# A masked cross-attention stage on one core: scores and side jobs share three PSUM banks instead of two and one, and a group's row maxima are turned one tile later

## What is computed

```python
def _L1_xattn_ref(q, k, v, mask, wq_w, wq_b, wk_w, wk_b, wv_w, wv_b, fo_w, fo_b):
    qp = (q @ wq_w.T + wq_b).reshape(N, -1, HEADS, HEAD_DIM)      # q: layernorm(x), 4 x 512 x 256, 16 heads of 16
    kp = (k @ wk_w.T + wk_b).reshape(N, -1, HEADS, HEAD_DIM)      # k, v: the context, 4 x 1601 x 256
    vp = (v @ wv_w.T + wv_b).reshape(N, -1, HEADS, HEAD_DIM)
    energy = jnp.einsum('nqhd,nkhd->nhqk', qp, kp)
    energy = jnp.where(mask == 0, jnp.float32(-1e+20), energy)
    attention = jax.nn.softmax(energy / np.float32(np.sqrt(EMBED)), axis=3)
    out = jnp.einsum('nhql,nlhd->nqhd', attention, vp).reshape(N, -1, EMBED)
    return out @ fo_w.T + fo_b
```

## Time and profile before

| | us |
|---|---|
| runs of the kernel before (3) | 2139.68, 2140.29, 2343.99; median 2140.29 |
| the profiled execution's own time | 2148.22 |
| its span in the trace | 2146.3 |
| masked attention in that span | 1103.3 to 1912.2 |
| PE busy over the span | 2006.8 (93%) |
| DVE, ACT, POOL busy over the span | 1270.2, 813.8, 527.3 |

### The profile page before, as it was taken

How to read it: one execution, slowest core, us unless ns; L and a number is a source line. 1 busy time by engine, 2 the same in 40 slices (tenths; PEclk the granted TensorE clock), 3 DMA queues, 4 the chain that set the end, 5 groups by cost and what they waited for, 6 DMA issues and landing times. The chain is left out here.

```text
span 2146.3 us, 27320 instructions
## 1 busy us (share of the span) xinstructions
PE 2006.8 (93%) x10237; PEld 1102.4 (51%) x10346; DVE 1270.2 (59%) x2541; ACT 813.8 (38%) x1631; POOL 527.3 (25%) x454
## 2 busy tenths in 40 slices
PE   8989999999999999899989999999999999974994
PEld 5666567746676567746643333333333343333773
DVE  5424764366544764477777777777777777641343
ACT  3412111211112111121127666666666766750221
POOL 4311001300010000000053132235324521326664
PEclk9999999999999999999999999999999999986997
DMA  8753000200011000200236473354335432224986
GB/s 284 210 199 109 0 1 17 70 10 1 1 37 45 1 1 11 46 16 31 31 103 111 132 213 65 79 134 107 89 70 145 103 56 39 64 71 147 257 186 157
DMA packets 101530, 184.97 MB, mean 86 GB/s; under 512 B 38151, under 2 KB 62549, under 8 KB 100120
## 3 DMA queue, kind: packets, MB, share of 16 engines
q1 hardware_dynamic: 83000, 153.24, 26.9%
q0 software_dynamic: 18400, 30.00, 6.0%
HBM read 127.38 MB, written 65.25 MB: 90 GB/s over the span
## 5 line engine op out<-in xcount | busy, mean ns | idle before, releaser
L2203 DVE CUSTOM_DVE_ANT_0 ps<-ps,maskN 128x801 f32<-128x801 f32 x480 | 468.4, 1014 | 179.8 <-PE ps L1987 174.2
L2176 ACT ACTIVATE d_prob<-ps 128x512 f32<-128x512 f32 (+1 forms) x832 | 460.5, 597 | 248.1 <-PE ps L2020 242.1
L856 PE MATMUL ps<-vx_or_keys,b_xT 128*128 128x512 f32 x512 | 240.3, 597 | 4.9 <-DVE val_or_prob L1209 4.9
L840 PE MATMUL ps<-oxB,og_or_pT 128*128 128x256 f32 x1024 | 241.1, 380 | 0.0
L2019 PE MATMUL ps<-maskT,identb 128*128 128x512 bf16 (+1 forms) x577 | 222.7, 386 | 1.9 <-ACT d_prob L2176 0.9
L2032 PE MATMUL ps<-d_prob,vaug 128*32 128x512 f32 (+1 forms) x1664 | 224.0, 604 | 0.3 <-ACT d_prob L2176 0.3
L840 PEld LDWEIGHTS ps<-oxB,og_or_pT 128*128 128x128 f32 x1024 | 190.5, 190 | 37.4 <-issue 11.2
L2019 PEld LDWEIGHTS ps<-maskT,identb 128*128 128x128 bf16 (+1 forms) x658 | 64.8, 99 | 260.0 <-ACT d_prob L2176 195.3
L1095 ACT ACTIVATE prob_or_gate<-ps,b_mx 128x512 f32<-128x512 f32 (+3 forms) x128 | 66.0, 524 | 289.5 <-DVE b_mx L1200 289.5
L260 POOL DMA_INDIRECT table<-xr,slot x128 | 127.8, 998 | 192.0 <-PE ps L2020 159.8
L1209 DVE TENSOR_TENSOR val_or_prob<-ps,b_gm 128x512 f32<-128x512 f32 x128 | 88.5, 691 | 107.0 <-PE ps L856 106.9
(11 more groups left out here) (321 smaller groups left out, 2801.9 us busy)
## 6 DMA issues: line engine op xcount, KB each, us to landing
c_rawT<-in_maskT SPq DMA_DIRECT2D x24, 512.0 KB
vx_or_keys<-k_parts SPq DMA_DIRECT2D x60, 200.1 KB, 7.3
k_parts<-x_k SPq DMA_DIRECT2D x16, 600.4 KB
table<-xr POOLq DMA_DIRECT2D x16, 578.0 KB
e_buf<-table SPq DMA_DIRECT2D x32, 289.0 KB
raw<-in_mask SPq DMA_DIRECT2D x10, 800.5 KB, 4.2
vx_or_keys<-in_D_w SPq DMA_DIRECT2D x12, 640.0 KB
e_w<-in_D_w SPq DMA_DIRECT2D x12, 640.0 KB
```

The lines of the kernel that those rows point to most:

```text
L840: mm = pe.matmul(ps[:, 6 + t // 2, (t % 2) * D:(t % 2 + 1) * D], og[:, e, t * P:(t + 1) * P], oxB[:, p, e, :], start=first and t % 2 == 0, ...
L856: mm = pe.matmul(ps[:, bank, :], xTB[:, c, t * P:(t + 1) * P], vxB[:, c, h, :], start=c == 0, stop=c == NC - 1)
L2176: nc.scalar.activation(prob[0:w, T % 2, h, :], ps[0:w, BANKS[GH * T + h], :], ACT.Exp, scale=SCALE_C).then_inc(exped, 1)
L2203: v.tensor_tensor_reduce(banks, banks, maskN[:, t, MO[half]:MO[half] + w], 1.0, -3.0e38, ALU.add, ALU.max, mp[:, t, h, half:half + 1]).the ...
```

## The change

`misc_jobs` and `score_plan` go, `bank_plan` takes their place: it walks through the stage in PE's order and gives each score and each side job the bank of 0, 1 and 3 (in group 15 also 6 and 7) whose last use began longest ago. A score or a job then waits for whatever reads that bank last: the exponential of the score, or the ACT or DVE read of the side job. With nothing between, score u of the stage waits for the exponential of score u - 3. After a side job that takes a bank behind tile i, scores 0 and 1 of tile i + 1 wait for the exponentials of scores 2 and 3 of tile i, and score 2 of tile i + 1 takes the job's bank and waits for the job's reads. ACT or DVE write a mask only into a bank that PE has written whole since its last side job; otherwise PE does. Walked through, the plan has the same numbers as before: 658 masks by PE, 150 by ACT, 24 by DVE. Group 15's first two scores use banks 6 and 7.

The one semaphore `freed` is split by reader (`freed_a`, `freed_v`). The waits of PE for `l_sub`, `carried` and the copy of "x" that guarded bank 3 stand now where the bank is used again. Two waits go: of score 2 of tile 11 for the last maximum's reduction, and of a group's second maximum for the exponentials. `turn_maxima` moves from behind score 3 of tile 11 to behind score 1 of tile 12.

```diff
+def bank_plan():
+    banks, before, masks, jobs, count, whole = [], [], [], {}, {"act": 0, "dve": 0}, set()
+    used, freed_by, reads, time = {}, {}, {"a": 0, "v": 0}, 0
+    def take(G, reader, after):
+        nonlocal time
+        bank = min((0, 1, 3) if G < NGB - 1 else (0, 1, 3, 6, 7), key=lambda x: used.get(x, x - 10))
+        free = freed_by.get(bank)
+        used[bank], freed_by[bank], time = time, (reader, after), time + 1
+        return bank, free
+    def job(G, name, reader, n=1):
+        bank, free = take(G, reader, reads[reader] + n)
+        whole.discard(bank)
+        jobs[name] = (len(jobs), bank, free, reader, reads[reader], n)
+        reads[reader] += n
...
+            for h in range(GH):
+                bank, free = take(G, "exp", len(banks) + 1)
+                banks.append(bank)
+                before.append(free)
                 by = "pe"
+                if bank in whole:
+                    if i >= 1 and G == NGB - 1 and h % 2:
+                        by = "dve"
+                    elif 1 <= i < NKT - 2 and G < NGB - 1 and h == GH - 1:
+                        by = "act"
+                elif KW[i] == P:
+                    whole.add(bank)
...
+        def bank_free(eng, free):
+            if free:
+                eng.wait_ge(READERS[free[0]], free[1])
...
                 if u == 0 and G >= 1:
                     pe.wait_ge(m_row, 2 * G)
-                if u == 1 and G >= 2:
-                    pe.wait_ge(exped, GH * NKT * (G - 1))
...
-                    if FREE[u]:
-                        pe.wait_ge(exped, FREE[u])
-                    if i == NKT - 2 and h == 2 and G + 1 < NGB:
-                        pe.wait_ge(mx_v, NM * (G + 2) - MADE)
+                    bank_free(pe, FREE[u])
...
                     score(T, 0)
                     score(T, 1)
+                    if i == NKT - 1 and G + 1 < NGB:
+                        turn_maxima(G + 1)
                     next_maximum()
...
                     score(T, 3)
                     next_maximum()
-                    if i == NKT - 2 and G + 1 < NGB:
-                        turn_maxima(G + 1)
...
                     if g == 1 and b >= 1 and i == 5:
                         read_of(pe, ("rt", b - 1, 1))
-                        r.logits(pe, MISC)
-                    if g == 1 and b >= 1 and i == 6:
-                        pe.wait_ge(r.l_sub, b)
+                        free_for(pe, ("logits", b - 1))
+                        r.logits(pe, bank_of(("logits", b - 1)))
...
                     if g == 1 and b >= 1 and i == 8:
-                        if b + 1 < NB:
-                            read_of(pe, ("x", b + 1, 1))
-                        r.counts(pe, MISC, b - 1)
-                    if g == 1 and b >= 1 and i == 9:
-                        pe.wait_ge(r.carried, b)
+                        free_for(pe, ("counts", b - 1))
+                        r.counts(pe, bank_of(("counts", b - 1)), b - 1)
```

More of the change, by code:

```diff
@@ L1610, in _, with seen @@
                                 ALU.add).then_inc(v_last, 1)
[L1613 to L1621, removed]
+def bank_plan():
[12 more added lines that the diff above has]
+        reads[reader] += n
+    def seen(G, name, reader, after):
+        bank, free = take(G, reader, after)
+        whole.discard(bank)
+        jobs[name] = (len(jobs), bank, free, reader, 0, 0)
     for G in range(NGB):
@@ L1625, in misc_jobs @@
         for i in range(NKT):
[L1626 to L1660, removed]
-                by = "pe"
[L1662 to L1665, removed]
+            for h in range(GH):
+                bank, free = take(G, "exp", len(banks) + 1)
+                banks.append(bank)
+                before.append(free)
+                by = "pe"
+                if bank in whole:
[5 more added lines that the diff above has]
+                    whole.add(bank)
                 if by != "pe":
@@ L1668, in score_plan @@
                 masks.append((by, count.get(by, 0)))
[L1669 to L1672, removed]
+            if i == 2 and G >= 1:
+                job(G, ("o", G - 1), "v", 2)
+            if g == 0 and b >= 1 and i in (4, 5):
+                job(G, ("ot", b - 1, i - 4), "a")
+            if g == 0 and b >= 1 and i in (7, 8):
+                job(G, ("f", b - 1, i - 7), "v", 2)
+            if g == 1 and b >= 1 and i in (3, 4):
+                job(G, ("rt", b - 1, i - 3), "a")
+            if g == 1 and b >= 1 and i == 5:
+                seen(G, ("logits", b - 1), "l_sub", b)
+            if g == 1 and b + 1 < NB and i in (6, 7):
+                job(G, ("x", b + 1, i - 6), "a")
+            if g == 1 and b >= 1 and i == 8:
+                seen(G, ("counts", b - 1), "carried", b)
+            if g == 1 and b + 1 < NB and i in (9, 10):
+                job(G, ("q", b + 1, i - 9), "a")
+            if G == NGB - 1 and i == 4:
+                job(G, ("ot", NB - 1, 0), "a")
+    job(NGB - 1, ("o", NGB - 1), "v", 2)
+    job(NGB - 1, ("ot", NB - 1, 1), "a")
+    return banks, before, masks, jobs
 def attention_c(k, A):
@@ L1690, in attention_c, with bank_of @@
     mask_a, mask_v = k.sem("d_mask_a"), k.sem("d_mask_v")
-    (ld_x, xb_done, split_q, biasN, biasT, ones, shared, freed, mx_mm, mx_v, neg, split_m, s_mm, exped,
+    (ld_x, xb_done, split_q, biasN, biasT, ones, shared, freed_a, freed_v, mx_mm, mx_v, neg, split_m, s_mm, exped,
      pv_mm, acc_ev, o_rec, f_last, x_last) = (
         k.sem("c_" + x) for x in (
[L1694 to L1700, removed]
+            "ld_x", "xb", "split_q", "biasN", "biasT", "ones", "shared", "freed_a", "freed_v", "mx_mm", "mx_v", "neg",
+            "split_m", "s_mm", "exp", "pv_mm", "acc_ev", "o_rec", "f_last", "x_last"))
+    ACC, LAST = 2, 4
+    SHARED = {name: n for n, name in enumerate(x for x in JOBS if x[0] not in ("logits", "counts"))}
+    def bank_of(name):
+        return JOBS[name][1]
     def filled_by(eng, name):
-        eng.wait_ge(shared, JOBS[name][0] + 1)
+        eng.wait_ge(shared, SHARED[name] + 1)
     def read_of(eng, name, reads=None):
-        _, before, all_of_it = JOBS[name]
-        eng.wait_ge(freed, before + (reads or all_of_it))
+        _, _, _, reader, before, all_of_it = JOBS[name]
+        eng.wait_ge((freed_a, freed_v)[reader == "v"], before + (reads or all_of_it))
     with ExitStack() as own:
@@ L2284, in _ @@
                     if g == 1 and u == 26 and b >= 1:
-                        r.places(v, MISC, b - 1)
+                        r.places(v, bank_of(("counts", b - 1)), b - 1)
                 if G + 1 < NGB:
```

38 lines of the change are left out of this document (21 added, 17 removed).

## The result

| | before | after |
|---|---|---|
| median of the runs, us | 2139.68 (5 runs) | 2122.92 (5 runs, 2119.93 to 2125.53) |
| ratio after/before, 95% interval | | 0.9934 [0.9923, 0.9946] |
| the profiled execution's own time | 2148.22 | 2119.93 |
| its span | 2146.3 | 2118.0 |
| first score of the masked attention | 1103.75 | 1100.85 |

The change takes 0.66% off, by the ratio about 14 us. The forecast was 11.6 us less than before, in a range of 1.3 to 23.3. One of the five runs of before took 2343.99 us; it stands in the median and not in the ratio.

What follows compares the result with a forecast made beforehand. PE was taken to bound the masked attention, with 24.9 us idle. Gains 5.7 + 1.9 + 5.3 + 3.1 = 16.0 less 1.2 + 2.0 + 1.2 = 4.4 gave 11.6 us: 2140.3 to 2128.7, range 2117 to 2139.

Steps and rivals of the forecast that it cites:

- rotation of three banks, tiles 1 to 10: Second scores of tiles, groups 0 to 14: 81 delays of 0.04 to 0.08 us vanish, 5.7 us gained.
- tile 0: Scores 2 and 3 of each group's tile 0: the same bank delays vanish, 1.9 us gained over the groups.
- ends of groups, less the new three-bank wait: Tiles 10 and 11: PE's waits for ACT vanish, 5.3 us gained; new wait at tile 11's score 3 costs 1.2.
- turn: waits won, less its new seams: Turn moved to tile 12: 3.1 us of waits for DVE's split gained, 0.13 in each of 15 groups, 2.0, paid.
- eaten by DVE in groups 2, 6, 10: Gains before DVE stalls at tiles 3 and 8 are lost again: 3 times 0.4, 1.2 us.
- Net zero at score 2 of tile 3: Groups 2, 6, 10: new 0.6 us wait for job "o" replaces 0.6 at a maximum; at worst 0.6 three times.
- The wait for the rows: Next group's first maximum behind the turn: DVE's copies finish with 0.4 us left, nothing charged; 9 us if they slipped.
- Rival A: DVE stalls swallow gains in all groups but those with g = 3: 7 us won, 2133; chance 0.16 with "nothing".
- Rival B: DVE's backlog falls elsewhere and the turn's seams are free: 20 us won, 2120; chance 0.14.
- Rival C: Score 2 behind 27 jobs read by DVE waits on the job's bank: slower, 2142 or 2169; chance 0.06.
- Rival D: PE's clock falls for a tile in each of 15 groups: 55 us less 12, 2184; chance 0.02.
- the signs: Right: quiet groups about 47.3, weight-load wait well below half, second score after 0.44; wrong: DVE-read waits, clock below 1.00.

Runs made afterwards that it cites:

- second profile of before: The kernel before, unchanged, run and profiled once more: 2136.53 us, ratio 1.0001, stage 808.1 us.
- turn_only: The kernel before with only the turn moved behind score 1 of tile 12, old bank plan: 2135.56 us, ratio 1.0001 to before, stage 807.9.
- banks_only: The changed kernel with the turn back at its old place behind score 3 of tile 11: 2125.89 us, ratio 0.9956 to before, stage 798.1.
- before_late_read: The kernel before with DVE's read of job "o" one maximum later: 2136.41 us, ratio 0.9999 to before, stage 810.0.
- second profile of after: The changed kernel, unchanged, run and profiled once more: 2122.64 us, ratio 0.9933 to before, stage 796.5 us.
- turn_placed: The changed kernel with the turn's place chosen group by group: 2123.93 us, ratio 0.9944 to before, stage 792.9.
- after_late_read: The changed kernel with DVE's read of job "o" one maximum later: 2135.60 us, ratio 0.9991 to before, stage 805.2.
- read_before_mask: The changed kernel with DVE's mask conversion put behind its read of job "o" in groups 2, 6, 10: 2126.07 us, ratio 0.9955 to before.

## Why the prediction was right, and where its terms were not

The time was forecast at 2128.7 and is 2122.9 in a range of 2117 to 2139: no change that the 2% bound would see, and about 14 us less where 11.6 was said. Of the 5.8 us between the two times 3 to 4 are the base and no term: the forecast started from 2140.3, the median of three runs, and the 21 runs that were timed twice later have 2136.06 and 2137.07. By terms, gained (+) and given back (-), over groups 0 to 14, from the distances between the starts of scores in both profiles:

| term | forecast | measured |
|---|---|---|
| rotation of three banks, tiles 1 to 10 | +5.7 | +5.9 |
| tile 0 | +1.9 | +1.8 |
| ends of groups, less the new three-bank wait | +5.3 - 1.2 | +4.5 |
| turn: waits won, less its new seams | +3.1 - 2.0 | -0.7 |
| eaten by DVE in groups 2, 6, 10, and what no term covers | -1.2 | +1.2 |
| group 15 | 0 | +0.5 |
| sum | 11.6 | 13.2 |

The same sums against the second profile of before differ in one row only, the last but two: +1.9. Of that 0.95 is in tile 10 of group 0 and 0.7 in tile 8 of group 2, where PE waits for DVE a varying time.

**The rotation** is as forecast, in place and size: all second scores that had been 0.04 to 0.08 late follow at 0.44. (There are 87 of them and not 81.) Where a side job stood between two tiles nothing had been late, so nothing was won. That is why groups 5 and 9, with a job behind nearly every tile, did not get shorter (56.4 and 56.5): they win 0.28 in tiles 0 to 2, and pay 0.13 for the three-bank wait and 0.25 for the turn.

**The ends of the groups** are right with the small wait that was said to come next. It shows as distances of 0.47 (1449.93 to 1450.40 above) and up to 0.52 where 0.44 is the least, 0.7 in sum where 1.2 was charged. Of the three groups that were to lose 0.5 to 0.9, one lost 0.45 and two 0.52.

**The turn** is the mis-sized term. Its waits of 3.1 went, as said. But "0.13 in each of 15 groups" was built on 0.88 for sixteen transposes and plain scores behind them. Measured, the next mask comes 0.98 after the turn's start, and its score 0.25 behind it instead of 0.22. In groups 5 and 7 the distance from tile 11's last score is 0.85 shorter and that across the new place 1.10 longer: 0.25 a group, and 3.75 for 15, inside the bounds that were given (0 to 4.5) but nearer to the upper one. So by the trace of before the turn should not have paid, and turn_only shows just that.

**What saved it** was not in the prediction as a term: the turn's waits were taken as those of the old PE, while the other parts of the change make PE arrive sooner by more than the split moves. In banks_only twelve groups stand there, up to 1.3 and 6.6 us in all, where before had three and 2.7. The gain of the move is what the rest of the change would have lost. Steps were costed each against the trace of before; these two had to be costed in order.

**"What is eaten"** holds in part. It said that what is won in groups 2, 6 and 10 before a DVE stall is lost again at that stall, 0.4 in each. Held against the second profile of before, groups 6 and 10 win 0.31 each at the second scores of tiles 5 to 8, and give back 0.15 at the stall in tile 6 and 0.08 at the one in tile 8. At tile 3 only 0.03 to 0.04 of what tiles 0 to 2 won is lost. That makes some 0.27 and not 0.4.

**What no term covers** is mostly not the change. In the table 1.26 of it is one place, the first score of tile 8 in groups 6 and 10: its second score came 0.83 and 1.31 behind it in the first profile of before and 0.44 after. In the second profile of before, in before_late_read and in turn_only, all with the old banks, it comes 0.51 behind. So 1.1 us of the stage's 13.2 belong to that one execution of before. The rest is steps of 0.03 and 0.11 at the ends of tiles, tile 0 above all, and 0.6 the other way in group 0. The turn came out 1.8 below its forecast and this row 2.4 above, and 1.1 of that by the chance of which execution was profiled: that the total is better than its parts is in good part luck.

**Net zero at score 2 of tile 3** holds in sum (0.65 longer there, 0.61 shorter at the maximum), and the experiment shows that 0.2 of it is a price of its own. **The wait for the rows** behind the turn was rightly charged with nothing: weight loads of the next group's first maximum wait up to 0.8 for DVE's copies in 14 groups, PE's matmuls in none.

**Rival A** fell: against the second profile of before, groups 4, 8 and 12 won 0.6 to 0.75 each and groups 6 and 10, with the longest DVE stalls, 1.5 each. **Rival B**'s price of 20 us was too high, though the seams went the other way than it said. **Rival C** did not come about, and the late read shows that it was one maximum away. **Rival D** did not come about: no kernel shows a fall of the clock in each group, and after has 1.00 from 1107 us to the end of the stage. But the mean of 1.00 hides two things. All ten profiles begin the stage at 0.50; in after PE had waited 5.35 us before the turn ahead of it, and the clock, 1.00 up to 1093, is 0.50 from 1097 to 1105. And in two profiles it fell within group 2, each time behind a wait for DVE at one maximum: of 1.75 us in the second profile of after, of 2.60 in before_late_read, which has the old banks. It stayed at 1.00 behind 1.94 in turn_only, 1.88 in turn_placed and 1.82 in the second profile of before. So it goes with neither plan of banks, and why it fell after 1.75 and not after 1.94 stays open. The Trainium skill, "TensorE: Matmul & The Clock Gate", section "A second HAM failure mode: psum-queue depth-cycling", describes a kernel that cycles through PSUM banks and falls back by short idle times between its matmuls; no run here shows that: even in after_late_read, where three masks waited 1.5 us for DVE, the clock was 1.00 behind them.

**Of the signs** that were named for being right, all held but one: the weight loads' wait of 195 us fell to 111.9, 57% of it, and not "well below half". The gaps that it was to stand for are gone all the same. It was a poor sign, since much of that wait costs PE nothing. Two of the signs for being wrong showed up in part: weight loads of 14 masks wait for DVE's L2252 (13.7 us), but PE itself in three of them, 1.7 us; and the clock fell for some 3 us in one of two profiles of after.

The timed gain of 14 is a little more than the 13 of the stage. The difference is within what one kernel varies, and part of it may lie ahead of the stage (last section).

## What to carry to other kernels

When one resource is shared in rotation by several kinds of work, list for each kind how late its reader is: a wait with half a microsecond to spare behaves as none, and a reader one instruction later can take back the whole gain. Cost the parts of a change in the order in which they make the bounding engine faster: a synchronization point that costs nothing now begins to cost once the engine arrives sooner, and moving it can be worth more beside the other parts than alone. Read gaps as distances between starts, since totals of hidden waits here fell by 43% or doubled with no such time behind them, and 7.9 us of the gain lay in what the profile calls busy. Check that both traces have all their records before two busy times are compared, and take a second profile of before: one place here was 1.1 us longer in the first alone.

## What the runs showed of the chip

A block of sixteen small transposes between two scores costs 0.25 us more than between a score and values: the distance between the two scores grows by 1.10, and the one at the old place shrinks by 0.85. Of the 1.10, the next mask comes 0.98 after the block's start, and that mask's score 0.25 behind it instead of 0.22. turn_placed shows the same the other way, by 0.1 to 0.3 a group.

A wait can cost more than its length. In group 2 of the second profile of after PE waited 0.6 us longer than in the first, and the clock that fell behind it took 1.6 more; in before_late_read it took 2.5.

The layers ahead of the change have the same code in all kernels, and yet they differ. The busy time by stretch from 100 to 200 and from 400 to 500 us shows it in the granted clock (the last figure but two). First the second profile of before:

```profile
100.00:200.00 100.00, 93.34 (x487) 66.03 (x486) 31.20 (x65) 21.06 (x39) 19.77 (x19) 0.98 0.48 175
400.00:500.00 100.00, 96.77 (x420) 56.78 (x420) 56.84 (x93) 21.97 (x57) 8.92 (x12) 0.97 0.12 40
```

and that of turn_only, which has the banks of before:

```profile
100.00:200.00 100.00, 93.33 (x476) 66.57 (x475) 30.46 (x64) 20.24 (x37) 19.77 (x19) 0.93 0.48 174
400.00:500.00 100.00, 96.77 (x438) 57.48 (x437) 58.62 (x93) 21.97 (x57) 10.01 (x13) 1.00 0.13 41
```

Both profiles of before and those of before_late_read, read_before_mask and after_late_read have 0.98 and then 0.97; their stages start at 1103.75, 1103.22, 1102.05, 1102.55 and 1105.37. Both profiles of after and those of banks_only, turn_only and turn_placed have 0.93 and then 1.00, and their stages start between 1100.85 and 1101.18. So two patterns exist, each with banks old and new and with the turn at either place, and with the second the stage begins 1 to 4.5 us earlier. That the clock is the cause was not tried. Some 2 us of the timed 14 may thus be this and not the change, and of the 3.4 us by which read_before_mask is slower than after, 1.6. What sets the pattern stays open.

By the load of the mask that group 2 waits for (800 KB), and by the clock where it fell behind that wait, the group took 49.6 in one execution of after and 51.8 in another, and 51.4, 51.8 and 55.2 in three of before, its late read included. A single profile's total can't carry a statement of less than some 4 us in such a kernel; groups and distances between starts can.
